# First attention of a two-block macaron network: VectorE takes over the group's end and two batches' stacks, and the bias goes through TensorE as float32r

## The reference

```
x = x + 0.5 * ffn0(layernorm(x))      # "f0", routed experts
x = x + attn0(layernorm(x))           # "a0", the stage that is changed
x = x + 0.5 * ffn0(layernorm(x))      # "g0"
x = x + 0.5 * ffn1(layernorm(x))      # "f1"
x = x + attn1(layernorm(x))           # "a1"
x = x + 0.5 * ffn1(layernorm(x))      # "g1"

# attn0: 16 heads of 8 channels
q, k, v = split(x @ w_qkv.T + b_qkv)
q, k = rope(elu(q) + 1), rope(elu(k) + 1)
out = softmax(q @ k.T / sqrt(8)) @ v                 # per head, 256 x 256
out = out + depthwise_conv3(v, w_lepe) + b_lepe      # over the tokens
```

## Time and profile before

| | before |
|---|---|
| median of 3 runs | 1391.83 us |
| the profiled execution, its own time | 1386.58 us |
| its span, first to last instruction | 1384.8 us |
| stage a0 in the span | 178.6 to 470.0 us |
| TensorE, VectorE, ScalarE, GpSimd busy over the span | 74%, 53%, 41%, 21% |
| mean granted TensorE clock | 0.817 of full |

### The profile page before, as it was taken

One profiled execution on the slowest core, in us unless ns is written; L12 is line 12 of the kernel. 1 busy time (PEld: TensorE's weight loads), 2 busy tenths in 40 slices (PEclk: granted clock), 3 DMA queues, 4 the chain that ended last, 5 costly groups with the idle time before them and its releaser, 6 DMA issues.

```text
span 1384.8 us, 24486 instructions
## 1 busy us (share of the span) xinstructions
PE 1029.7 (74%) x7716; PEld 760.0 (55%) x7716; DVE 733.2 (53%) x2468; ACT 567.6 (41%) x1399; POOL 289.4 (21%) x339
## 2 busy tenths in 40 slices
PE   3798936888899659988209962799999999613992
PEld 2346824555555434567208952567666676512992
DVE  6866864455433377677601226477667777530222
ACT  3113632444433320146103422377777777501440
POOL 2103056221100030020263541000000000044552
PEclk9799975778755579999558985699999999856996
DMA  7003000000000330210747638544554442455652
GB/s 207 0 0 104 0 14 0 1 1 1 1 1 1 96 82 0 66 39 0 137 124 202 190 108 249 166 147 144 153 153 118 134 134 74 81 128 145 189 159 92
DMA packets 168539, 126.07 MB, mean 91 GB/s; under 512 B 16451, under 2 KB 151387, under 8 KB 168436
## 3 DMA queue, kind: packets, MB, share of 16 engines
q1 hardware_dynamic: 163444, 116.25, 30.9%
q0 software_dynamic: 4992, 8.54, 1.7%
HBM read 85.89 MB, written 40.69 MB: 91 GB/s over the span
## 4 chain that ended last, share of the span: by engine, by line
PE 59%; DVE 20%; issue 10%; SPq 3%; ACT 3%; DMA 2%; POOL 1%; POOLq 0%; DVEq 0%; PEld 0%; ACTq 0%; PEldq 0%
PE psum L415 6%; PE psum L424 6%; PE psum L763 5%; PE psum L848 4%; PE psum L1409 4%; PE psum L1362 3%; PE psum L211 3%; PE psum L1854 3%; PE psum L1866 2%; PE psum L1896 2%; PE psum L1327 2%; PE psum L167 2%; PE psum L1886 2%; PE psum L213 2%; PE psum L835 2%
## 5 line engine op out<-in xcount | busy, mean ns | idle before, releaser
L1544 DVE TENSOR_REDUCE a_negmax<-psum 128x2 f32<-128x512 f32 x128 | 86.1, 688 | 120.3 <-PE psum L1362 120.3
L990 DVE TENSOR_TENSOR g_S<-g_place,g_number 128x512 bf16<-128x512 f32 (+1 forms) x116 | 76.7, 702 | 17.0 <-PEq L758 6.0
L1487 ACT ACTIVATE a_PT<-psum 128x1024 f32<-128x1024 f32 x64 | 65.5, 1023 | 46.9 <-PE psum L1394 45.3
L1362 PE MATMUL psum<-a_turned 24*128 24x256 f32 x256 | 75.5, 400 | 7.5 <-DVE a_negmax L1544 7.4
L451 ACT ACTIVATE f_hT<-psum,f_b 128x256 f32<-128x256 f32 x92 | 37.3, 470 | 98.4 <-PE psum L415 98.4
L451 ACT ACTIVATE g_hT<-psum,g_b 128x256 f32<-128x256 f32 x92 | 37.3, 470 | 97.3 <-PE psum L415 97.3
L990 DVE TENSOR_TENSOR f_S<-f_place,f_number 128x512 bf16<-128x512 f32 (+1 forms) x100 | 66.2, 704 | 14.2 <-PEq L758 6.2
L1971 ACT ACTIVATE a_pr<-a_L,a_least 128x128 f32<-128x128 f32 x128 | 50.7, 396 | 55.1 <-DVE a_least L2031 55.1
L1362 PEld LDWEIGHTS psum<-a_turned 24*128 24x128 f32 x256 | 49.0, 248 | 27.1 <-issue 15.4
L1973 ACT ACTIVATE a_pr<-a_L,a_least 128x256 f32<-128x256 f32 x128 | 63.5, 496 | 0.0
L1409 PE MATMUL psum<-a_PT,a_Vs 128*32 128x256 f32 x512 | 51.7, 540 | 15.4 <-DVE a_attn L1578 15.4
(11 more groups left out here) (500 smaller groups left out, 2743.3 us busy)
## 6 DMA issues: line engine op xcount, KB each, us to landing
a_z<-a_G SPq DMA_DIRECT2D x32, 512.0 KB, 3.1
a_X<-a_z SPq DMA_DIRECT2D x16, 1024.0 KB, 6.9
f_w<-in_W SPq DMA_DIRECT2D x46, 256.0 KB
g_w<-in_W SPq DMA_DIRECT2D x46, 256.0 KB
a_X<-a_z SPq DMA_DIRECT2D x16, 512.0 KB, 3.8
f_wgu<-in_gate_up SPq DMA_DIRECT2D x16, 384.0 KB, 6.5
g_wgu<-in_gate_up SPq DMA_DIRECT2D x16, 384.0 KB, 4.7
a_z<-a_pad SPq DMA_DIRECT2D x6, 1024.0 KB, 8.6
```

What stands on the lines that cost most here:

```text
L990: return dve.tensor_tensor(S[:, slot, :].rearrange("p (t e n) -> p t e n", t=1, n=CAPACITY), bcast(place[:, ds(t, 1), CE * k:CE * k + CE], ...
L1362: last = pe.matmul(bank[h % 2][:, SEQ * t:SEQ * t + SEQ], q[rows, g, P * t:P * t + P].bitcast(F32R), k[rows, g, :].bitcast(F32R), start=Tr ...
L1544: dve.tensor_reduce(negmax[:, :, h], bank[h % 2].rearrange("p (t n) -> p t n", n=SEQ), AX.X, ALU.max, negate=True).then_inc(max_done, 1)
```

## The change

Three edits, all in `attention_zero`:

- `take_out` moves from ScalarE to VectorE, and on VectorE `finish` and `take_out` now stand between the two maxima of a step instead of behind them (`finish`) or on ScalarE (`take_out`).
- The biases are split in two float32r parts (`high_part`, `rest_part`) instead of three bfloat16 parts, `bias_rows` and `edge` become float32, and the three bias matmuls take float32r operands. The q, k, v bias gets a semaphore of its own (`bias_loaded`), and its first split now stands ahead of the convolution's diagonals. The memsets of `edge` and `Vs` go behind the layer norm. TensorE's L1428 and ScalarE's copy of `lepe_rows` go from behind the third to behind the first of the last three quarters.
- The stacks of batches 0 and 1 are made by VectorE, behind each batch's rope. GpSimd keeps those of the others. The semaphore `roped` goes, and `elus` waits for `stacked` instead.

```diff
     def gpsimd(pool):
...
+            full, high, low, rows = (m[:, first:end, :] for m in (bias, bias_high, bias_low, bias_rows))
+            step(high_part(pool.tensor_copy, high, full))
+            step(rest_part(pool, low, full, high))
+            pool.tensor_scalar(high, high, core.ident[:, 0:1], None, ALU.mult)
+            step(pool.tensor_scalar(low, low, core.ident[:, 1:2], None, ALU.mult))
+            pool.tensor_tensor(rows.bitcast(F32R), high, low, ALU.add).then_inc(done, 1)
...
+        pool.wait_ge(bias_loaded, 16)
+        step(pool.tensor_copy(bias[:, 0:2, :], bqkv[:, 0:2, :]))
+        split_bias(0, 2, qk_bias_ready)
         pool.wait_ge(lepe_loaded, 32)
         for j in range(4):
             pool.tensor_scalar(diag[:, j, :], core.ident[:, :], wl[:, j:j + 1] if j < 3 else bl[:, 0:1], None,
                                ALU.mult).then_inc(diag_ready, 1)
-        pool.wait_ge(loaded, 4 * 16)
-        step(pool.tensor_copy(bias[:, 0:2, :], bqkv[:, 0:2, :]))
-        split_bias(0, 2, qk_bias_ready)
+        pool.wait_ge(ln.xn_ready, TILES)
+        step(pool.memset(edge[:, :, :], 0.0))
...
-        stacks(0)
-        stacks(1)
         value_weights()
...
     def tensor(pe):
...
-                last = pe.matmul(out[:, :, t, :], core.ones[:, :], bias_rows[:, 0:2, :], start=False, stop=True,
+                last = pe.matmul(out[:, :, t, :], ones_f[:, :].bitcast(F32R), bias_rows[:, 0:2, :].bitcast(F32R), start=False, stop=True,
...
-                last = pe.matmul(out[:, 1, t, :], edge[:, t, :], bias_rows[:, 4 + t, :], start=False, stop=True,
+                last = pe.matmul(out[:, 1, t, :], edge[:, t, :].bitcast(F32R), bias_rows[:, 4 + t, :].bitcast(F32R), start=False, stop=True,
...
     def scalar(act):
...
-            if group_of(n, 3) is not None:
-                take_out(group_of(n, 3))
...
     def vector(dve):
...
             if b < 2:
                 dve.wait_ge(elu_ready, b + 1)
-                dve.wait_ge(loaded, 4 * 16)
-                rope(dve, b, step).then_inc(roped, 1)
+                dve.wait_ge(loaded, 3 * 16)
+                step(rope(dve, b, step))
+                stacks(dve, b, step).then_inc(stacked, 1)
...
+        def take_out(m):
+            dve.wait_ge(pv_done, m + 1)
+            if m >= 2:
+                dve.wait_ge(o_turned, m - 1)
+            dve.tensor_copy(OT[m % 2][:, :], bank[VB][:, 0:SEQ]).then_inc(o_copied, 1)
...
+            if group_of(n, 4) is not None:
+                finish(group_of(n, 4))
+            if group_of(n, 3) is not None:
+                take_out(group_of(n, 3))
             if due[1]:
                 maximum(*due[1])
             if u == 7 and inside(i + 1):
                 take_shift(i + 1)
-            if group_of(n, 4) is not None:
-                finish(group_of(n, 4))
```

More of the change, by code:

```diff
@@ L1197, in rope, with stacks @@
         return eng.tensor_tensor(z[s][:, :, :], z[s][:, :, :], rot[s][:, :, :], ALU.add)
+    def stacks(eng, b, step):
+        s = b % 2
+        q, k = (stack[s][:, a, :, :, :].rearrange("p t h d -> p (t h) d") for a in range(2))
+        for a, m in enumerate((q, k)):
+            full = z[s][:, 2 * a:2 * a + 2, :].rearrange("p t (h d) -> p (t h) d", d=D0)
+            view = m[:, :, 0:PARTS].rearrange("p n (i d) -> p n i d", d=D0)
+            last = high_part(eng.tensor_copy, view[:, :, 0:2, :] if a == 0 else view[:, :, 0:3:2, :],
+                             full.unsqueeze(2).to_broadcast([P, 2 * H0, 2, D0]))
+        step(last)
+        for a, m in enumerate((q, k)):
+            full = z[s][:, 2 * a:2 * a + 2, :].rearrange("p t (h d) -> p (t h) d", d=D0)
+            at = 2 * D0 if a == 0 else D0
+            last = rest_part(eng, m[:, :, at:at + D0], full, m[:, :, 0:D0])
+        return last
     def gpsimd(pool):
@@ L1222, in gpsimd @@
             pool.memset(m[:, :, :, :, PARTS:HW].rearrange("p a t h d -> p (a t h) d"), 0.0).then_inc(filled, 1)
-        pool.memset(edge[:, :, :], 0.0)
         step(pool.memset(head[:, :], 0.0))
-        for i, last in ((0, 0), (1, P - 1)):
-            pool.memset(edge[:, i, last:last + 1], 1.0).then_inc(filled, 1)
         for part in range(2):
@@ L1287, in gpsimd @@
             pool.wait_ge(stacked, b - 1)
-            rope(pool, b, step).then_inc(roped, 1)
-            stacks(b)
+            step(rope(pool, b, step))
+            pool.wait_ge(tk_done, 4 * (b - 1))
+            stacks(pool, b, step).then_inc(stacked, 1)
     def tensor(pe):
@@ L1488, in probabilities @@
                            core.psum[:, 2 + 2 * (u % 2):4 + 2 * (u % 2), :], ACT.Exp, scale=SCALE).then_inc(p_ready, 1)
-        def take_out(m):
-            act.wait_ge(pv_done, m + 1)
-            if m >= 2:
-                act.wait_ge(o_turned, m - 1)
-            copy(OT[m % 2][:, :], bank[VB][:, 0:SEQ]).then_inc(o_copied, 1)
         ln.deviation(act)
```

61 lines of the change are left out of this document (18 added, 43 removed).

## The result

The changed kernel takes 1351.64 us (median of 4 runs, 1350.94 to 1353.01) against 1390.72 us before (4 runs, 1386.60 to 1392.36): ratio 0.9725, 95% interval 0.9701 to 0.9748. That is 39 us less; the forecast was 1371 us, 1357 to 1383. The profiled execution took 1351.6 us, with a span of 1349.9 and a mean granted clock of 0.835. Stage a0 lies from 183.72 to 439.57 us in it, 255.9 us instead of 291.4 us.

A forecast was written before the change was run, and what follows sets the result against it. The prediction took TensorE, with its waits and its clock, to bound the stage. 3.6 + 4.8 + 12.0 - 2.0 + 2.5 = 20.9 us off the median of 1391.83 gave 1370.9, say 1371 us; range 1357 to 1383 (8 in 10).

The forecast's parts named there:

- the clock: TensorE's granted clock: a little more of the full clock, 2.5 us gained, anything from -15 to +15.
- rival B: TensorE's clock turns kinder, two or three batches won: 10 us more gain, 1360 us; chance 0.15.
- The sign set for the clock: Forecast wrong if a batch in the loop's middle has a mean granted clock outside 0.7 to 0.95.
- The waits: TensorE's idle time at the start, before the values' weights and in the loop: 3.6 + 4.8 + 12.0 us gained.
- The start: First projection 5.6 us earlier, VectorE's first maximum 3.6 us earlier; with the 4.8 us at the values' weights.
- the values' weights: TensorE's wait of 4.83 us before L1342 for GpSimd's second bias split goes whole, with 9 us of cover.
- Rival E: VectorE's new stacks take the start's whole gain: 3.6 us less, 1375 us; inside the forecast's 0.50.
- The loop: 27 waits of TensorE for the group's end before the values shrink or go: 12.0 us gained.
- rival A: VectorE becomes the loop's bound, the 27 waits give 5 us instead of 12: 1378 us; chance 0.20.
- The float32r bias: TensorE's bias matmuls keep their rate, 16 edge corrections take 0.12 instead of 0.06 us: 2.0 us lost (0 to 5).
- Rival C: Edge corrections cost four passes and lost fast weight loads appear: 6 us worse, 1377 us; chance 0.07.
- Rival D: Full clock lost in all six batches that had it, 5 us each: 1401 us; with partial forms, chance 0.08.

The follow-up runs named there:

- start_only: The changed kernel with `take_out` back on ScalarE and `finish` behind the second maximum again: 1393.90 us, ratio 1.001 against the kernel before.
- stack1_pool: The changed kernel with the second batch's stack back on GpSimd: 1356.66 us, ratio 0.974 against the kernel before.
- takeout_only: The kernel before with only `take_out` moved to VectorE, in front of the second maximum, `finish` still behind it: 1389.52 us, ratio 0.999.
- finish_only: The kernel before with only `finish` moved in front of the second maximum, `take_out` left on ScalarE: 1356.70 us, ratio 0.978.
- fill_late: The changed kernel with one more overwritten bfloat16 matmul in each step of batches 5 to 7: 1370.21 us, ratio 0.984 against the kernel before.

## Why the prediction was wrong, point by point

**The step that failed: the clock.** It said "I expect a little more of the full clock: 2.5 us", within -15 to +15. It gave 15.7 us of busy time. The mechanism was named, and rival B ("the clock turns kinder", 10 us more, 1360) had its sign, but the term was mis-sized: I took a tenth of one batch's 27 us, without a price for a batch between the two levels. Rival B's price, 5 us a batch, compared windows with different work (x189 and x210 records) at 0.55 and 0.88. What stood in the trace of before and was not used is that the last batch alone had half clock throughout, with 22.93 us of busy time (its last window above), of which the full clock could save up to half; it saved 9.8 us. The range's lower end, 1357 us, was B's middle, too near. The sign set for the clock, a batch in the loop's middle outside 0.7 to 0.95, did not show: stretches 2 to 6 have 0.70 to 0.93, and much of the gain lay in the last batch. The sign of the term could not have been foreseen, as start_only and stack1_pool show: edits of the start, which left less idle time, moved the busy time by +7.5 and +13.4 us against the kernel they started from. The range had to hold both. Another 3.5 us of the miss lie in no trace: the forecast was 20.9 us under the median, the measured medians are 39.1 apart, the profiled stages 35.6.

**The waits: right in sum.** Forecast 20.4 us, idle time 19.9 us less. The loop gave 13.8 us (stretches 1 to 8: 32.8 us idle before, 19.1 after) for 12.0, the start 6.2 us for 8.4. That the sum is so near is partly luck: an error of +1.8 us and one of -2.2 cancel.

**The start: 8.4 forecast, 5.3 came.** The first projection, 8.85 us into the stage and let go by ScalarE's copy, and the values' weights without a wait came as forecast. The first maximum did not: 26.24 us into the stage before, 208.90 - 183.72 = 25.18 after, 1.06 us earlier instead of 3.6. The first stack took 2.8 us and the second 3.2, against 2.2 forecast for each, and the second rope 3.6 us against 2.8; together that is the 2.5 us that are missing. The term at fault is the price of VectorE's work: it was taken from rows in which GpSimd was idle (196.79 to 198.9 us before), while GpSimd now works beside it. The first stack lost it in the subtractions (0.85 us each instead of 0.38), the second in the casts (1.06 each). Rival E was so nearly true in its result, though its own numbers, 4.4 us new against 5.6 us, leave 1.2 us of gain and not none. The estimate from the Trainium skill, VectorE: DVE Perf Modes, section Mode 2×_2P — use both read ports for one tensor (0.42 us a copy), was under both measured values, 0.58 and 1.06; no run shows such a copy without GpSimd at work. The rule that bore on this step is another: the Trainium skill, SBUF — State Buffer, section SBUF: two separate sides, says that VectorE and GpSimd share a pair of ports under an exclusive lock, which a VectorE operation needs if it streams one tensor through both ports or, against a GpSimd operation that reads SBUF, if it reads two tensors from there, and that the later one is blocked for the whole of the other's instruction. The slowed rows agree: the subtractions end at 202.13 us, just behind GpSimd's product (200.68 + 1.17 us), and the casts at 207.81, just behind its subtraction (206.21 + 1.32 us). stack1_pool showed the price of the second stack, 3.7 us.

**The loop: right.** Idle before L1402 1.5 us (forecast under 3), before L1381 7.5 (near 7). That before L1355 grew by 4.0 us over the stage, above the 3 us set for rival A; but all of that lies in stretch 0, where the wait behind the second stack stands (5.02 us). Behind stretch 0 it is 4.5 us in both kernels, and with the loop's edit alone it was 7.5 over the stage, as before. A did not happen. That the copy on VectorE is of any use was assumed; takeout_only and finish_only show that it is not needed.

**The float32r bias: 2.0 us forecast, nothing came.** At full clock one batch's values and convolution ran from 313.49 to the next scores at 315.85, 2.36 us; before from 369.85 to 372.19, 2.34. The correction has its 0.06 us. At other clocks it is as free: stretch 5 took 30.71 us with 26.59 busy at 0.72 before, and stretch 4 of start_only, which has the float32r bias, took the same. Rival C is out. The Trainium skill, TensorE: Matmul & The Clock Gate, section Weight-path perf modes — Fast Weight Load (FWL) and DoubleRow, denies the fast load to float32. The loads agree (for L1340 222 ns in the mean after, for L1347 122 ns before, float32r against bfloat16), but they lay beside other matmuls and cost nothing.

**Rival D** did not happen in the changed kernel, but start_only is near to it in its result: the start shifted, three batches at 0.72 instead of two, and the whole gain gone. Whether it came about as D says, by the full clock missing the work of the projection, was not shown.

**Still open.** What in the order of busy and idle pieces lets the full clock start or end was not settled, and the split in busy and idle time rests on one execution of each kernel, while their times spread by up to 20 us. The forecast of a single kernel's clock could not be made from these runs.

## What to carry to other kernels

Split a stage's time into idle and busy time of the bounding engine, for the same records, before and after: the idle part of an edit adds up and can be forecast, the busy part goes with the clock and can be as large, with either sign. Price it by the same batch at either level before setting the range. And where TensorE waits a little at the same place in each batch, a few overwritten matmuls of the full array in that wait are a cheap trial: here they were worth 22 us. The same number spread over the steps of three batches made the kernel 19 us slower, but 4 us of that arose in a batch without any of them. Before adding work, look for one call in the wrong place: `finish` in front of the second maximum was worth 35 us.

## What the runs showed of the hardware

- Lengths repeat to 0.01 us over batches and over kernels: 27.21 to 27.23 us at 0.75 in the changed kernel (two batches), stack1_pool (three) and fill_late (three), 30.71 and 30.72 at 0.72 in start_only. finish_only, with other waits, had 27.19 and 27.18. In these kernels batches with the same mixture of the two levels follow each other; in the kernel before they alternate, 0.88, 0.72, 0.88, 0.72.
- The last batch, x156 records, is 28.21 us at 0.50 and 18.46 at 1.00. At full clock too it is TensorE's for most of its length: TensorE works without a wait from 421.44 to 432.6 us, and ScalarE waits 0.70 us for it between each two pairs of exponentials. Then TensorE waits for the ends of the last groups, 0.5 to 0.7 us each time, and the stage's last 3.3 us have no matmul.
- VectorE's cast of 512 elements in runs of 8 to float32r took 0.58 us in the mean beside GpSimd's products of the values' weights, and 1.06 beside its bias split; the subtractions of 256 elements 0.85 and 0.57.
- The time outside the stage, in which all kernels are the same, fell into two groups, both before the stage (178.5 to 180.7 and 183.2 to 184.3 us) and behind it (909.4 to 911.0 and 914.6 to 916.0 us), over 17 traces.
- A float32r matmul over 128 columns followed by others costs 0.06 us at full clock, the same as in bfloat16.
